# A gated attention and expert layer on one core: first-step transfers from two queues, sums shared by two engines, a filled wait and new order tables

## What is computed

```python
x = x + tanh(g_xattn) * xattn(layernorm(x), ctx)
    q_hk  = (hidden_q @ Wq.T);  q_big = einsum('bshk,hkq->bshq', q_hk, w_kc_q)      # 192 wide
    q_big = rope(q_big);        kv_r  = rope(kv_c)                                 # kv 64 wide
    q_r   = einsum('bshq,hqr->bhsr', q_big, W_qr);  k_r = einsum('bld,hdr->bhlr', kv_r, W_kr)
    attn  = softmax(q_r @ k_r)
    ctx   = einsum('bhsl,bld->bhsd', attn, kv_r) -> w_kc_kv -> Wo
x = x + tanh(g_ffn) * ffn(layernorm(x))
    scores = softmax(x @ router.T + bias);  w, idx = top_k(scores, 8)
    ffn    = x * sum(w) + einsum('tk,tkh->th', w, expert_bias[idx])
```

## Time and profile before

| | before |
|---|---|
| time, median of 3 runs | 266.04 us (264.98 to 266.11) |
| the profiled execution | 266.02 us, of which the span is 264.2 us |
| busy, of the span | PE 94%, DVE 68%, ACT 55%, POOL 53% |
| mean granted clock of TensorE | 0.982 of full speed |

### The profile page before, as it was taken

The page is one execution under the profiler, slowest core; times in us unless marked ns, Lnnn a source line. Parts: engine busy times, 40 slices in busy tenths (PEclk is TensorE's granted clock), DMA queues, the critical chain, the costliest instruction groups (busy, mean ns, idle before and its releaser), DMA issues.

```text
span 264.2 us, 5591 instructions
## 1 busy us (share of the span) xinstructions
PE 248.3 (94%) x1921; PEld 185.1 (70%) x1921; DVE 178.9 (68%) x434; ACT 144.2 (55%) x440; POOL 139.5 (53%) x223
## 2 busy tenths in 40 slices
PE   7995999999999999999999999999999989789982
PEld 7782578668775878577867876787668657667761
DVE  3798588757684767676657944777568546665675
ACT  2811366674645566556555456556553567767531
POOL 3649039722793177419652592448624942535552
PEclk9997799999999999999999999999999999999997
DMA  7967534373000051303300300020003000000112
GB/s 235 243 164 191 177 68 113 106 227 79 2 0 2 11 129 50 125 8 79 94 0 2 79 4 0 19 65 1 2 0 82 1 2 0 1 2 0 40 43 81
DMA packets 17852, 16.72 MB, mean 63 GB/s; under 512 B 5152, under 2 KB 16544, under 8 KB 17824
## 3 DMA queue, kind: packets, MB, share of 16 engines
q1 hardware_dynamic: 17280, 15.90, 22.8%
q10 hardware_dynamic: 544, 0.46, 0.5%
HBM read 11.11 MB, written 1.05 MB: 46 GB/s over the span
## 4 chain that ended last, share of the span: by engine, by line
PE 82%; DVE 4%; ACT 4%; DMA 3%; issue 3%; POOL 3%; SPq 2%; POOLq 0%; DVEq 0%; ACTq 0%
PE ring L1093 23%; PE probs_t L1254 13%; PE scores L1243 11%; PE context L1272 10%; PE ring L1132 6%; PE ring L1059 4%; PE ring L1118 3%; PE ring L1153 2%; PE ring L1149 2%; PE ring L1151 2%; DMA w_kc_q_sb<-in_w_kc_q 2%; ACT probs L760 2%; PE ring L1082 1%; PE ring L1073 1%; POOL roped L594 1%
## 5 line engine op out<-in xcount | busy, mean ns | idle before, releaser
L657 POOL TENSOR_SCALAR probs<-probs,inv_sum 128x256 f32<-128x256 f32 x128 | 60.1, 485 | 96.2 <-DVE inv_sum L1004 96.0
L770 ACT COPY probs_t_sb<-probs_t 128x512 f32<-128x512 f32 x64 | 37.6, 588 | 60.6 <-PE probs_t L1254 60.5
L760 ACT ACTIVATE probs<-scores,neg_max 128x256 f32<-128x256 f32 x128 | 59.9, 477 | 3.0 <-DVE neg_max L998 2.9
L587 POOL TENSOR_TENSOR roped<-roped,cross 128x512 f32<-128x512 f32 x31 | 39.2, 1289 | 10.0 <-DVE cross L849 10.0
L998 DVE TENSOR_REDUCE neg_max<-scores 128x2 f32<-128x512 f32 x64 | 40.9, 680 | 2.6 <-PE scores L1243 2.4
L1254 PE MATMUL probs_t<-ident,probs 128*128 128x128 f32 x256 | 40.4, 280 | 1.6 <-ACT probs_t_sb L770 1.0
L1093 PE MATMUL ring<-xn_hi,a_hi 128*128 128x512 f32 x96 | 41.0, 427 | 0.3 <-DVE xn_lo L832 0.3
L848 DVE TENSOR_TENSOR roped<-ring,rope_q_sb 128x512 f32<-128x512 f32 x48 | 32.8, 683 | 7.6 <-PE ring L1093 7.2
L1093 PE MATMUL ring<-xn_hi,a_lo 128*128 128x512 f32 x96 | 37.8, 393 | 0.0
L1093 PE MATMUL ring<-xn_lo,a_hi 128*128 128x512 f32 x96 | 37.5, 390 | 0.0
L1254 PEld LDWEIGHTS probs_t<-ident,probs 128*128 128x128 f32 x256 | 28.5, 140 | 11.5 <-issue 3.5
(11 more groups left out here) (107 smaller groups left out, 466.2 us busy)
## 6 DMA issues: line engine op xcount, KB each, us to landing
moved<-cross SPq DMA_DIRECT2D x32, 128.0 KB, 2.3
wo_t_sb<-in_wo_t SPq DMA_DIRECT2D x4, 512.0 KB, 4.1
w_qr_sb<-in_w_qr SPq DMA_DIRECT2D x4, 384.0 KB, 4.5
wq_sb<-in_wq SPq DMA_DIRECT2D x3, 512.0 KB, 4.0
w_kc_q_sb<-in_w_kc_q SPq DMA_DIRECT2D x3, 384.0 KB, 4.7
x_sb<-in_x SPq DMA_DIRECT2D x3, 256.0 KB, 5.5
out<-x_sb SPq DMA_DIRECT2D x3, 256.0 KB, 2.1
wq_sb<-in_wq SPq DMA_DIRECT2D x2, 256.0 KB, 4.7
```

The lines of the kernel that those rows point to most:

```text
L587: last = nc.gpsimd.tensor_tensor(roped[:, j, k, :], roped[:, j, k, :], cross[:, k, j, :], ALU.add)
L657: last = nc.gpsimd.tensor_scalar(e, e, inv_sum[:, i % 4, half:half + 1], 1.0, ALU.mult, ALU.mult)
L760: last = nc.scalar.activation(probs[:, i % E_BUFS, half, :], scores[:, i % 2, half, :], ACT.Exp, bias=neg_max[:, i % 4, half:half + 1], ac ...
L770: nc.scalar.copy(probs_t_sb[:, i % T_BUFS], probs_t[:]).then_inc(probs_t_ready, 1)
```

## The change

1. In the first step SyncE issues only quarters 0 and 1 of the swap; a new piece ("hand",) lets ScalarE issue quarters 2 and 3, behind its copy of the keys and ahead of the third table copy.
2. In the first step GpSimd adds only one half of `moved` and the sums of block 1. VectorE adds the other half of `moved` and, in one instruction, both halves of block 2 (`first_sums`). The semaphores that TensorE and VectorE wait on follow that.
3. TensorE turns the identity 8 times ahead of ("r", 0), 8 times ahead of ("x", 1, 0) and 4 times in the middle of it (`FILLED_WAITS`).
4. The order tables are laid out anew: the pieces before the first item, all steps but the sixth (n = 5), and the pieces after the last item. Of the step tables those of steps n = 3, 4, 6 and 7 are shown below, each between brackets of its own.

```diff
+FILLED_WAITS = {('r', 0): 8, ('x', 1, 0): 8, ('x', 1, 0, 2): 4}
...
 def pieces_before():
-    return [("n", 0), ("a", 0, 0), ("a", 0, 2), ("x", 0, 0), ("x", 0, 1), ("a", 0, 1), ("a", 0, 3), ("table", 0),
-            ("half", 2), ("c",), ("q", 0, 0, 0), ("q", 0, 0, 1), ("q", 0, 1, 0), ("q", 0, 1, 1), ("table", 1),
-            ("move", 0), ("q", 0, 2, 0), ("table", 2), ("q", 0, 2, 1), ("k", 0), ("m", 0, 0), ("n", 1), ("r", 0),
-            ("p", 0), ("x", 1, 0), ("x", 1, 1)]
+    return [("n", 0), ("a", 0, 1), ("a", 0, 0), ("c",), ("a", 0, 2), ("x", 0, 0), ("a", 0, 3), ("x", 0, 1),
+            ("half", 2), ("table", 0), ("q", 0, 0, 0), ("table", 1), ("q", 0, 0, 1), ("q", 0, 1, 0), ("k", 0),
+            ("move", 0), ("q", 0, 1, 1), ("q", 0, 2, 0), ("hand",), ("q", 0, 2, 1), ("table", 2), ("m", 0, 0),
+            ("r", 0), ("n", 1), ("p", 0), ("x", 1, 0), ("x", 1, 1)]
 def pieces_at_start():
-    return [("q", 1, 0, 0), ("q", 1, 0, 1)]
+    return [("q", 1, 0, 0)]
...
     (
-        ([("q", 4, 1, 1), ("centre",)], []),
-        ([("q", 4, 2, 0)], [("o", 2, 0), ("move", 4)]),
-        ([], [("out", 2, 0, 2)]),
-        ([("q", 4, 2, 1)], [("a", 3, 3)]),
-        ([("out", 2, 2, 2)], []),
-        ([("r", 4), ("p", 4)], [("q", 5, 0, 0), ("a", 3, 0)]),
+        ([("centre",), ("q", 4, 1, 1), ("move", 4)], []),
+        ([("q", 4, 2, 0)], []),
+        ([("o", 2, 0), ("q", 4, 2, 1)], [("out", 2, 0, 2)]),
+        ([], [("out", 2, 2, 2)]),
+        ([("a", 3, 3)], [("r", 4), ("p", 4)]),
+        ([("q", 5, 0, 0)], [("a", 3, 0), ("q", 5, 0, 1)]),
         ([], []),
-        ([("q", 5, 0, 1), ("q", 5, 1, 0)], [("q", 5, 1, 1), ("a", 3, 2)]),
+        ([("a", 3, 2), ("q", 5, 1, 0), ("move", 5)], [("q", 5, 1, 1)]),
     ),
     (
-        ([("move", 5), ("q", 5, 2, 0)], [("out", 3, 4, 2), ("a", 3, 1)]),
-        ([("q", 5, 2, 1)], [("m", 3, 0)]),
+        ([("q", 5, 2, 0)], [("a", 3, 1), ("q", 5, 2, 1)]),
+        ([("out", 3, 4, 2)], [("m", 3, 0)]),
         ([], []),
         ([("out", 3, 6, 2)], [("r", 5), ("p", 5)]),
-        ([("q", 6, 0, 0)], []),
-        ([("q", 6, 0, 1)], []),
-        ([("o", 3, 0)], [("out", 4, 0, 2)]),
-        ([], [("q", 6, 1, 0), ("move", 6)]),
+        ([], [("q", 6, 0, 0), ("q", 6, 0, 1)]),
+        ([], []),
+        ([("o", 3, 0)], [("out", 4, 0, 2), ("move", 6)]),
+        ([], [("q", 6, 1, 0)]),
     ),
...
     (
-        ([("q", 7, 1, 1), ("q", 7, 2, 0), ("move", 7)], []),
-        ([("q", 7, 2, 1), ("out", 5, 4, 2)], []),
-        ([("r", 7)], []),
+        ([("q", 7, 1, 1)], [("q", 7, 2, 0), ("move", 7)]),
         ([], []),
-        ([("p", 7)], [("out", 5, 6, 2)]),
+        ([("q", 7, 2, 1), ("out", 5, 4, 2)], [("r", 7)]),
+        ([], [("p", 7)]),
+        ([], [("out", 5, 6, 2)]),
         ([], []),
         ([], [("out", 6, 0, 2)]),
-        ([("root", 0, 2)], []),
+        ([], [("root", 0, 2), ("turn", 0, 2)]),
     ),
     (
-        ([("turn", 0, 2)], [("logit", 0, 2)]),
-        ([("gate", 0, 2)], [("take", 0, 2)]),
-        ([], [("out", 6, 2, 2)]),
-        ([("turn", 2, 2)], [("pick", 0, 2), ("root", 2, 2)]),
-        ([("logit", 2, 2), ("gate", 2, 2)], [("take", 2, 2)]),
-        ([], []),
-        ([("part", 0, 2), ("out", 7, 4, 2), ("root", 4, 2)],
-         [("mix", 0, 2), ("turn", 4, 2), ("gate", 4, 2), ("pick", 2, 2)]),
-        ([], [("logit", 4, 2), ("take", 4, 2)]),
+        ([], [("logit", 0, 2)]),
+        ([], [("take", 0, 2)]),
+        ([("gate", 0, 2)], [("out", 6, 2, 2)]),
+        ([("root", 2, 2), ("turn", 2, 2)], [("gate", 2, 2)]),
+        ([("pick", 0, 2), ("logit", 2, 2)], [("take", 2, 2)]),
+        ([("part", 0, 2)], []),
+        ([("out", 7, 4, 2)], [("mix", 0, 2), ("turn", 4, 2)]),
+        ([("root", 4, 2), ("pick", 2, 2)], [("part", 2, 2), ("logit", 4, 2)]),
     ),
...
 def pieces_after():
-    return [("part", 2, 2), ("pre", 7, 6, 2), ("part", 4, 2), ("out", 7, 6, 1), ("root", 6, 1), ("out", 7, 7, 1),
-            ("root", 7, 1), ("pick", 4, 2), ("turn", 6, 1), ("mix", 2, 2), ("gate", 6, 1), ("turn", 7, 1),
-            ("logit", 6, 1), ("logit", 7, 1), ("take", 6, 1), ("mix", 4, 2), ("gate", 7, 1), ("part", 6, 1),
-            ("take", 7, 1), ("pick", 6, 1), ("part", 7, 1), ("mix", 6, 1), ("pick", 7, 1), ("mix", 7, 1)]
+    return [("take", 4, 2), ("gate", 4, 2), ("part", 4, 2), ("pre", 7, 6, 2), ("out", 7, 6, 1), ("out", 7, 7, 1),
+            ("pick", 4, 2), ("turn", 6, 1), ("mix", 2, 2), ("turn", 7, 1), ("root", 6, 1), ("root", 7, 1),
+            ("gate", 6, 1), ("gate", 7, 1), ("logit", 6, 1), ("logit", 7, 1), ("take", 6, 1), ("take", 7, 1),
+            ("part", 6, 1), ("mix", 4, 2), ("part", 7, 1), ("pick", 6, 1), ("pick", 7, 1), ("mix", 6, 1),
+            ("mix", 7, 1)]
...
-        def swap_quarters(queue):
-            for quarter in range(4):
+        def swap_quarters(queue, quarters=range(4)):
+            for quarter in quarters:
...
-                    swap_quarters(sp)
+                    swap_quarters(sp, range(4) if piece[1] else (0, 1))
...
             def rope_sums(n, k, u):
                 pool.wait_ge(ring_free, freed[u])
-                for j in range(1 if n == 0 and k == PC - 1 else 2):
+                for j in range(2):
                     last = nc.gpsimd.tensor_tensor(roped[:, j, k, :], roped[:, j, k, :], cross[:, k, j, :], ALU.add)
                 last.then_inc(rope_ready, 1)
             def add_moved(n):
                 pool.wait_ge(moved_in, 64 * (n + 1))
-                for j in range(2):
+                for j in range(2 if n else 1):
...
-                    if piece[0] == "q" and piece[3] == 1 and piece[2]:
+                    if piece[0] == "q" and piece[3] == 1 and piece[2] and piece[1:3] != (0, PC - 1):
                         rope_sums(piece[1], piece[2], u)
...
-                    if kind == "table":
+                    if kind == "hand":
+                        act.wait_ge(ring_free, freed_by[("q", 0, 0, 1)])
+                        swap_quarters(act, (2, 3))
+                    elif kind == "table":
...
                 if j == 0 and n:
-                    if k:
-                        dve.wait_ge(rope_ready, 2 * n - 2 + k)
-                    else:
+                    if k == 0:
                         dve.wait_ge(moved_sums, n)
+                    elif n > 1 or k == 1:
+                        dve.wait_ge(rope_ready, max(1, 2 * n - 3 + k))
+                    if n == 1:
+                        dve.wait_ge(shared_sum, 2)
...
+                    first_sums(u)
+            def first_sums(u):
+                dve.wait_ge(moved_in, 64)
+                nc.vector.tensor_tensor(roped[:, 1, 0, :], roped[:, 1, 0, :], moved[:, 1, :], ALU.add
+                                        ).then_inc(shared_sum, 1)
+                dve.wait_ge(ring_free, freed[u])
+                nc.vector.tensor_tensor(roped[:, :, PC - 1, :], roped[:, :, PC - 1, :], cross[:, PC - 1], ALU.add
+                                        ).then_inc(shared_sum, 1)
...
+            def idle_turns(count):
+                for _ in range(count):
+                    nc.tensor.transpose(scores[:, 0, 0, 0:P], ident[:], ident[:])
...
+                    if i == 2:
+                        idle_turns(FILLED_WAITS.get(("x", t, dc, i), 0))
...
                 pe.wait_ge(moved_sums, n + 1)
+                if n == 0:
+                    pe.wait_ge(shared_sum, 1)
...
-                pe.wait_ge(rope_ready, 2 * n + 2)
+                pe.wait_ge(rope_ready, 2 * n + 1)
                 if n == 0:
-                    pe.wait_ge(shared_sum, 1)
+                    pe.wait_ge(shared_sum, 2)
...
+                    idle_turns(FILLED_WAITS.get(piece, 0))
                     free(u)
```

More of the change, by code:

```diff
@@ L38 @@
 WARM_UP = 24
+FILLED_WAITS = {('r', 0): 8, ('x', 1, 0): 8, ('x', 1, 0, 2): 4}
 LEAD = 2
-NO_BANK = ("n", "c", "table", "move", "root", "gate", "take", "part", "pre", "half")
+NO_BANK = ("n", "c", "table", "move", "hand", "root", "gate", "take", "part", "pre", "half")
 FREED_BY_SCALAR = ("m", "turn", "pick")
@@ L60, in pieces_before @@
 def pieces_before():
[L62 removed]
[3 rows of a table removed]
+    return [("n", 0), ("a", 0, 1), ("a", 0, 0), ("c",), ("a", 0, 2), ("x", 0, 0), ("a", 0, 3), ("x", 0, 1),
[3 rows of a table added]
 def pieces_at_start():
[L70 removed]
+    return [("q", 1, 0, 0)]
 STEP_SLOTS = (
     (
[L75 to L79 removed]
+        ([("a", 1, 1), ("q", 1, 0, 1)], []),
+        ([("q", 1, 1, 0)], [("move", 1)]),
+        ([("o", 0, 0), ("q", 1, 1, 1)], [("a", 1, 3), ("q", 1, 2, 0)]),
+        ([("q", 1, 2, 1)], [("k", 1), ("m", 1, 0), ("o", 1, 0)]),
+        ([], [("a", 1, 2)]),
         ([("r", 1), ("p", 1)], [("a", 1, 0)]),
[L81 to L86 removed]
+        ([], []),
+        ([("q", 2, 0, 0)], []),
+    ),
+    (
+        ([("q", 2, 0, 1)], [("a", 2, 3), ("q", 2, 1, 0)]),
+        ([("out", 0, 0, 2)], [("move", 2)]),
         ([], []),
         ([("q", 2, 1, 1), ("q", 2, 2, 0)], [("q", 2, 2, 1), ("out", 0, 2, 2)]),
```

(19 more changed lines are left out.)

19 lines of the change are left out of this document (1 added, 18 removed).

## The result

| kernel | median, us | lowest and highest, us | ratio to the kernel before (95% interval) |
|---|---|---|---|
| before | 266.01 | 263.49 to 267.21 (20 runs) | 1 |
| after | 267.33 | 265.48 to 268.41 (20 runs) | 1.0054 (1.0033 to 1.0074) |

The change makes the kernel slower, by 0.54%; the forecast was 264.0 us, and the time lies above the range. The profiled execution of the kernel after took 268.24 us, 266.4 us of it span; it is the second longest of the twenty, 0.9 us above the median.

A forecast was written before the change was run, and what follows sets the result against it. TensorE's own work was taken to bound 40 to 240 us, leaving the start and the end. 266.0 - 0.5 (start) - 0.6 (tables) - 0.9 (end) = 264.0 us, range 262.2 to 265.7 us.

The forecast's parts named there:

- Part 1: First step: swap issued from two queues, sums shared, identity turned; gain 0 to 1.1 us, taken as 0.5 us.
- the landing of the last quarter: First step's swap: 2.2 to 3.2 us to land, last quarter there at 19.1 to 20.1 us, taken as 19.7.
- Transfers: First step's swap: two quarters issued by ScalarE, so the last one is there 0.9 us sooner.
- Sums taking turns: First step: GpSimd's and VectorE's adds alternate instead of running side by side; layer norm starts at 24.3 to 25.4 us.
- The clock: Start, before the second rank queries: in a wait of up to 2.6 us the clock may fall.
- The turns: TensorE at the start: identity turns stand in waits and cost nothing; up to 1.9 us if the later ones' cover goes.
- Tables: New order tables from the steps on: 0.6 us gained in the steps and 0.9 us at the end.
- the end: From about 206 us: two scalings moved later, roots 1.0 us sooner; gain 0.9 us, bounds 0.3 and 1.2.
- part 2: Step tables: rank queries between two turns of probabilities cover step 6's 0.77 us wait; gain 0.6 us, bounds -0.3 and 0.8.
- slower, GpSimd held up by its own queue: Steps 4 to 6: earlier moved adds delay scaling, TensorE waits 1.4 us at up to three steps; 268.2 us, chance 0.09.

The follow-up runs named there:

- e2_tables_only: The kernel before with only the new step and end tables, its pieces at the start, sums and swap kept; 264.24 us, ratio 0.9934.
- e1_front_only: The kernel after with the step and end tables of the kernel before, so only the start is new; 268.33 us, ratio 1.0074.
- e5_loads_held: The kernel after, with SyncE holding back its weight loads until all four swap quarters have landed; 267.04 us, ratio 1.0058.

## Why the prediction was wrong

The step that failed is Part 1. It was to gain 0.5 us; by the kernel after against e2_tables_only (267.33 and 264.24 us) it lost 3.1 us, so it was 3.6 us off, somewhat more than the whole distance between 264.0 and 267.3 us. The term that failed first is the landing of the last quarter, 19.7 us in the sum and 21.87 us in the trace; the place of the block-1 sums behind it, put at nothing, made it dear.

- *Transfers: wrong.* I took the landing time of a quarter as a constant of 2.2 to 3.2 us and subtracted issue time. With two queues the second of ScalarE's landed late (5.0 us), and the step as a whole is no shorter: 5.7 us from first issue to use, against my 19.7 us minus a first issue at about 15.6 us, 4.1 us. Only e1_front_only shows the 4.2 us (landing at 19.76 us), and there the rest of Part 1 came about as forecast: layer norm from 23.79 us, second rank queries from 25.09 us, the projection 1.19 us sooner. What the last quarter waited for elsewhere is, by the packets, a load of program code. In the kernel before that load met an earlier quarter (3.2 us, the longest in the earlier trace rows) and was over when the last was issued; issued sooner, the last quarter ran into it.
- *Sums taking turns: right in the mechanism, wrong in what it delays.* VectorE's long sum took 2.29 us beside GpSimd. By the rule of the Trainium skill that I had weighed ("SBUF — State Buffer", section "Who interferes with whom") this was to be expected, and these traces agree: 1.23 us alone and 2.29 us beside GpSimd's adds. The layer norm started at 24.71 us, within the forecast 24.3 to 25.4, but by luck: the landing was 2.2 us late, and the layer norm began 2.8 us behind it, where I had 4.4 to 5.6 us. VectorE's moved half went first (21.89 us), so only one of GpSimd's adds came between its two sums. But I had put the second rank queries at 25.3 to 25.6 us. They hang on GpSimd's last sum, which ended at 27.1 us, since every add stands behind the landing: 2.2 us of late landing are 1.6 to 1.9 us of late rank queries. I had written that "the block-1 sums are no longer done during the wait" and priced it at nothing, counting only that three adds stayed three. With a late landing it was the dearest edit of the change: putting these sums ahead of the landing again gave 3.7 us.
- *The clock: right as a risk, wrong as a price.* I had named a wait of up to 2.6 us before the second rank queries, in which the clock may fall. It was 2.18 us, the clock fell behind it, and I had put it at a smaller gain, never at a loss. The equal wait without a fall in e1_front_only shows it as a risk and no more.
- *The turns: the cover was gone.* The twelve later turns were to hide behind the layer norm. The rank queries ended later than the last normalising did (29.36 us), so these turns stood in front of ready work, eight of them at half clock (1.65 us) and four more (0.60 us). My 1.9 us "if that cover is gone" was about the right size for their length and stood outside the sum; all twenty, with what they do for the clock, cost 0.66 us by the medians.
- *Tables: right in sum, partly by luck, and not in parts.* e2_tables_only gained 1.2 to 2.3 us, 1.5 were forecast. In the traces the rest from the first projection to the last addition fell from 229.93 us (230.12 in e1_front_only) to 228.8 to 229.0 in all but two of the twelve kernels with the new tables, 1.1 us. All of it is the end (from the last turn of probabilities on 13.92 us before, 12.8 to 13.0 after; 0.9 were forecast). The wait of 0.77 us in step 6 is gone, TensorE's waits for copies of probabilities fell from 1.0 to 0.3 us in the run, but up to that last turn no time was saved: part 2 gave nothing, within its bounds. TensorE's waits there fell by 0.65 us in all, and its busy time rose by as much (from 211.6 to 212.25 us in e2_tables_only) with the same instructions; why is open. The other 0.7 us between the profiled executions of e2_tables_only and before are no work of the tables: the start has the same pieces in both, and the clock was low there for 3 us instead of 6.
- *The rival "slower, GpSimd held up by its own queue"* named a real mechanism (the wait of 0.71 us ahead of step 5, behind a swap that landed late), at a sixth of the price. It appears in the kernel after and in e5_loads_held alone (rest 229.61 and 230.14 us). No rival had the start itself slower; the time came between my bound of 266.0 us and this rival's 268.2 us, for the most part for another reason than it gives.

## What to carry to other kernels

When work moves from ahead of a wait to behind it, count it in full on whatever waits for the last of it, even if the number of instructions behind the wait stays the same: an engine's idle time ahead of a late transfer is where its ready work belongs. Fillers that are to keep the clock up cost time here behind a late producer, where they were work in front of work; where the wait was sure they gained by the medians, and where it was longer than they are they changed nothing. And a landing time read from one trace holds for what else the DMA engines did at that moment: when an issue moves, ask what it will meet.

## What the runs showed of the hardware

- A swap of four times 128 KB within SBUF was usable 5.2 to 5.9 us after its first issue, from one queue (issues of 2.5 to 3.35 us) and from two (1.2 and 1.5 us), with 4.2 us once; halving the issue time did not shorten it.
- A 16 KB packet of program code took 0.9 to 1.8 us, and a swap of which a 4 KB packet began as such a packet ended had its slowest quarter land 2.68 to 5.18 us after its issue (47 of 112 swaps); without that it took at most 2.64 us, but for one of 3.46 us.
- VectorE's sum of 128x1024 from two SBUF inputs took 1.23 us beside an idle GpSimd and 2.29 us beside its adds; GpSimd's add took 1.27 us alone and 1.76 us beside VectorE's. VectorE's two sums of the first step took 2.98 us together in either order.
- One program ran with different granted clocks: e1_front_only took 264.98 us once, at a mean of 0.992 and with 1.00 throughout the start, and 267.80 to 268.84 us ten times, at means of 0.979 to 0.988.
